# All nine depthwise taps of a convolution block on TensorE as 64x64 matmuls

## The chip, the cores and the metric

The kernel runs on one core of a Trainium2 chip. The metric is the device time of one execution in microseconds (us). A core has five engines that run side by side and meet at semaphores: TensorE (PE, matmuls and transposes, results to PSUM; PEld is its loading of weights), VectorE (DVE), ScalarE (ACT), GpSimd (POOL) and SyncE (SP), which here only issues DMA.

## The reference

The input x is 16 images of 128 channels and 28x28 pixels, all float32.

```
x = x + conv(layer_norm_over_channels(x))
   conv: h = depthwise 3x3(h) + dw_b;  h = relu(bn1(h)); a channel of an image whose max is below 4.0 becomes 0
         h = pointwise 128x128(h) + pw_b; h = relu(bn2(h)); a channel whose max is below 0.001 becomes 0
t = tokens of x: 12544 rows of 128
t = t + ffn(layer_norm_over_the_row(t))
   ffn: softmax over all tokens of t @ Wr (8 experts); each expert takes its 1024 best tokens;
        gelu(sel @ W1 + b1) @ W2 + b2, weighted with the probability, added back at the tokens' places
```

## The kernel before

There are three phases. The first, up to 213 us, takes the 16 images through norm, convolution and the routing logits; the second is a search for each expert's threshold among the tokens; the third gathers rows, runs the experts and scatters and adds. The change touches only the first.

An image lies in SBUF with channels on the 128 partitions. The first phase is a software pipeline written out by hand: `steps` calls each engine's `step(pair, u)` once for each image and some more to fill and drain, and in a step the engine works on several images, each at another stage. `image(pair, u, lag)` gives the image at a stage: lag 0 is the newest, lag 5 the oldest. Steps 6 to 13 are a hardware loop with two steps in its body, the others are written out. Semaphore counts are all that order the engines.

The stages of an image are: PE transposes it to tokens in seven tiles of 112 (L704), DVE takes statistics (L964) and small moments (L976 to L1001), ACT norms the seven tiles into `ln_tok` (L538), PE transposes them back (L769) into `psB`, ACT copies them in two parts into `x_pad`, an image with a border of zeros (L570). Then comes the depthwise convolution. A tap is one of the nine shifts of the 3x3 window. Four taps run on PE (L691): for each half of the image (14 lines, 392 pixels) four matmuls of a 128x128 diagonal matrix with the shifted view of `x_pad` add up in `psC`. Five taps run on DVE (L1009): the first per half, adding the sum in `psC` (128x392), the other four over the whole image in `conv` (128x784).

ACT then applies batch norm and relu (`act1`, L519) and sums signs to find dead channels (L509). DVE turns the sum into a flag (L1077) and masks the pointwise weights with it (`pw_masked`, L1085). PE does the pointwise product (L729), ACT norms it (`act2`, L492) and sums signs (L500), DVE adds the residual (`x1`, L1103). PE transposes `x1` to token rows in `psD` (L746) and makes the logits (L750). DVE takes statistics of the rows, ACT norms seven tiles of them (L483), and SP stores them. Matmuls of float32 appear in the trace as two records each, one after the other, and each with a weight load of its own; a transpose is one record.

On SP each step loads the input for two images later, the residual's input and a store of zeros, and stores finished rows.

## Time and profile before

| | |
|---|---|
| median of 3 runs (504.53 to 506.65) | 505.8 us |
| profiled execution, from first to last instruction | 502.9 us |
| PE, PEld busy | 361.9, 255.7 us |
| DVE, ACT, POOL busy | 327.1, 274.3, 159.3 us |
| mean granted TensorE clock | 0.857 |

The profiled execution has no timed figure of its own, only its span. What lies around the span can be taken as 2.9 us, the median less the span. A row of a group gives how often an operation ran, its busy time, the mean length of one, and the idle time in front. [...] In a timeline several instructions of one line are merged, so the time from one to the next is the length less one instruction, divided by their number less one. Matmuls are pipelined, so that a record is longer than the distance to the next.

### The profile page before, as it was taken

The numbers are of one execution on the slowest core, as the hardware profiler recorded it, in microseconds if no ns is written. First come the engines' busy times: TensorE is split into PE (matmuls) and PEld (weight loads), VectorE is DVE, ScalarE is ACT, GpSimd is POOL, SyncE is SP. The second block draws the span as 40 slices with busy tenths as digits, with TensorE's granted clock in tenths as the row PEclk, the third lists the DMA queues.
The fourth block names the chain that finished last, engine by engine and source line by source line (L and its number), as shares of the span: only waits on it lengthen the run. The fifth ranks groups of instructions, "written<-read, shape, count | busy, mean of one in ns | idle before, by whom it ended". The sixth has DMA issues, their size and how long they took to land. (4 is left out here: it accounts for less than half of the span.)

```text
span 502.9 us, 6936 instructions
## 1 busy us (share of the span) xinstructions
PE 361.9 (72%) x1947; PEld 255.7 (51%) x1947; DVE 327.1 (65%) x1004; ACT 274.3 (55%) x587; POOL 159.3 (32%) x151
## 2 busy tenths in 40 slices
PE   4989888888889985631021798999990498876575
PEld 3656555566666553520011374677560467464453
DVE  5699988888889898578879548556620025235444
ACT  3577888888888876677640528556551240510000
POOL 4000000000000000000005777787888788876000
PEclk9999999999999997655555799999997598997755
DMA  4604555555554342479101223344443267847998
GB/s 103 188 38 141 185 168 185 167 185 168 185 182 150 130 131 96 137 238 392 71 1 33 55 56 94 95 65 64 83 85 34 55 189 134 194 61 169 285 390 344
DMA packets 36396, 72.01 MB, mean 143 GB/s; under 512 B 6385, under 2 KB 16785, under 8 KB 36369
## 3 DMA queue, kind: packets, MB, share of 16 engines
q1 hardware_dynamic: 24256, 56.52, 35.0%
q0 software_dynamic: 9472, 8.66, 11.2%
q10 hardware_dynamic: 2640, 6.51, 3.3%
q8 instruction: 12, 0.20, 0.2%
q14 instruction: 16, 0.12, 0.1%
HBM read 34.96 MB, written 30.29 MB: 130 GB/s over the span
## 5 line engine op out<-in xcount | busy, mean ns | idle before, releaser
L403 POOL DMA_INDIRECT picked<-token_rows,slot_idx x32 | 31.5, 986 | 270.7 <-issue 270.4
L691 PE MATMUL psC<-x_pad,tap_diag 128*128 128x392 f32 x256 | 90.8, 498 | 6.7 <-ACT x_pad L570 5.6
L1009 DVE SCALAR_TENSOR_TENSOR conv<-x_pad,taps_w,conv 128x784 f32<-128x784 f32 x64 | 65.9, 1030 | 0.8
L691 PEld LDWEIGHTS psC<-x_pad,tap_diag 128*128 128x128 f32 x256 | 46.1, 189 | 37.0 <-DVE conv L1009 5.1
L1302 DVE TENSOR_TENSOR y_sum<-psC,b_rows 128x512 f32<-128x512 f32 x15 | 10.4, 692 | 75.2 <-PE psC L869 75.2
L869 PE MATMUL psC<-w,hid 128*128 128x128 f32 x480 | 56.6, 280 | 2.2 <-ACT hid L633 2.1
L869 PEld LDWEIGHTS psC<-w,hid 128*128 128x128 f32 x480 | 55.8, 197 | 4.6 <-issue 3.0
L613 ACT ACTIVATE picked_T<-psA 128x512 f32<-128x512 f32 x16 | 9.0, 594 | 59.9 <-PE psA L836 59.9
L426 POOL DMA_INDIRECT moe_sum_late<-y_rows,slot_idx x24 | 37.9, 1581 | 9.5 <-issue 7.0
L483 ACT ACTIVATE rows<-psD,sm 112x128 f32<-112x128 f32 x98 | 35.7, 464 | 9.3 <-DVE sm L1001 9.3
L729 PE MATMUL psB<-act,pw_masked 128*128 128x392 f32 x64 | 27.9, 563 | 17.0 <-DVE pw_masked L1085 17.0
L426 POOL DMA_INDIRECT moe_sum<-y_rows,slot_idx x24 | 37.8, 1573 | 7.3 <-issue 7.0
L633 ACT ACTIVATE hid<-psB,b_T 128x512 f32<-128x512 f32 x32 | 21.7, 685 | 31.3 <-PE psB L857 31.3
L538 ACT ACTIVATE ln_tok<-psA,sm 112x128 f32<-112x128 f32 x98 | 36.0, 501 | 0.8 <-DVE sm L1001 0.8
L857 PE MATMUL psB<-picked_T,w 128*128 128x512 f32 x64 | 32.3, 629 | 4.9 <-ACT picked_T L613 3.9
L857 PE MATMUL psC<-picked_T,w 128*128 128x512 f32 x64 | 32.2, 614 | 0.0
L964 DVE BATCH_NORM_STATS2 st<-psD 112x6 f32<-112x128 f32 x112 | 24.8, 286 | 9.5 <-PE psD L750 7.9
L633 ACT ACTIVATE hid<-psC,b_T 128x512 f32<-128x512 f32 x32 | 21.8, 687 | 15.1 <-PE psC L857 15.1
L729 PEld LDWEIGHTS psB<-act,pw_masked 128*128 128x128 f32 x64 | 12.0, 206 | 31.0 <-DVE pw_masked L1085 19.1
L797 PE MATMUL psA<-sign_sum,half_same 128*128 128x4 f16 x16 | 3.0, 188 | 34.2 <-ACT x_in L585 33.2
L964 DVE BATCH_NORM_STATS2 st<-psA 112x6 f32<-112x128 f32 x105 | 22.2, 285 | 5.6 <-PE psA L704 5.6
L1199 DVE TENSOR_SCALAR_CACHE_REDUCE conv<-dist,cand 128x784 bf16<-128x784 f32 (+1 forms) x31 | 24.6, 830 | 0.9 <-DVE cand L1217 0.5
(211 smaller groups left out, 728.8 us busy)
## 6 DMA issues: line engine op xcount, KB each, us to landing
token_rows<-rows SPq DMA_DIRECT2D x16, 416.5 KB, 3.6
x_in<-in_x_dram SPq DMA_DIRECT2D x16, 392.0 KB, 3.5
x_res<-in_x_dram SPq DMA_DIRECT2D x16, 392.0 KB, 4.3
moe_sum<-zero_rows SPq DMA_DIRECT2D x16, 392.0 KB, 4.9
x_all<-x SPq DMA_DIRECT2D x16, 392.0 KB, 2.9
moe_sum_late<-zero_rows SPq DMA_DIRECT2D x16, 392.0 KB, 7.7
out_dram<-act ACTq DMA_DIRECT2D x16, 392.0 KB, 6.2
w<-in_L_ffn_W_dram SPq DMA_DIRECT2D x16, 256.0 KB, 3.3
```

The lines of the kernel that those rows point to most:

```text
L403: nc.gpsimd.indirect_dma_start(out=picked_in[k][:, b, :], out_offset=None, in_=rows_dram, in_offset=bass.IndirectOffsetOnAxis(ap=slot_idx[ ...
L426: nc.gpsimd.indirect_dma_start(out=sums, out_offset=at, in_=y_rows[:, q, b, :], in_offset=None, compute_op=ALU.add).then_inc(s_sca[q], 16)
L483: ins = nc.scalar.activation(rows[:, q5, t * ROW:t * ROW + C], row_region(img5)[:, t, :], ACT.Identity, bias=row_sm[:, 6, t:t + 1], scale= ...
L538: ins = nc.scalar.activation(ln_tok[:, q, t * C:(t + 1) * C], ln_region(img)[:, t, :], ACT.Identity, bias=ln_sm[:, 6, t:t + 1], scale=ln_s ...
L633: nc.scalar.activation(hid[:, f, h * HS:(h + 1) * HS], hidden_bank[f], ACT.Gelu, bias=b1_T[:, ds(e * FT + f, 1)]).then_inc(s_gelu, 1)
L691: ins = nc.tensor.matmul(psC[:, h, 0:HALF].rearrange("c (h w) -> c h w", w=W), tap_diag[:, n, :], x_pad_v[:, q, y0:y0 + LINES, dx:dx + W], ...
L729: nc.tensor.matmul(psB[:, h, 0:HALF], pw_masked[:, q, :], act1[:, q, h * HALF:(h + 1) * HALF], start=True, stop=True).then_inc(s_pw, 1)
L857: nc.tensor.matmul(hidden_bank[f], w1[:, q, f * 128:(f + 1) * 128], picked_T[:, h * HS:(h + 1) * HS], start=True, stop=True).then_inc(s_l1, 1)
L869: ins = nc.tensor.matmul((psA if first else psC)[:, h, b * C:(b + 1) * C], hid[:, f, lo:lo + 128], w2[:, q, f * C:(f + 1) * C], start=(f = ...
L964: ins = nc.vector.bn_stats(st[:, lo + t, :], region[:, t, :])
L1009: return nc.vector.scalar_tensor_tensor(o, x_pad_v[:, q, y0 + dy:y0 + dy + lines, dx:dx + W], taps_w[:, PE_TAPS + n:PE_TAPS + n + 1], acc, ...
L1199: return nc.vector.tensor_scalar(junk[:, column, 0:n], dist[:, 0:n], value.bitcast(F32), -offset, ALU.is_lt, ALU.add, accum_out=cnt[:, col ...
```

## The change

The five taps on DVE and their buffers' waits go. All nine taps run on PE as 64x64 matmuls. The 128 channels are split into two halves of 64. For the upper 14 lines of the image the two halves of the channels use rows 0 to 63 of the array with columns 0 to 63, and rows 64 to 127 with columns 64 to 127. For the lower 14 lines the input lies in SBUF with the two channel halves exchanged, and the matmuls use the two other quarters of the array (rows 0 to 63 with columns 64 to 127, and the reverse), so that the result comes out at the right partitions. For each tap the four quarters follow one another: 36 matmuls per image, each over 392 pixels, where there were 8.

To have the lower half exchanged, `x_pad` becomes two parts of 17 lines. ACT copies the first 16 lines straight (L525 of the kernel after), and DVE copies the last 16 lines in two instructions, each from 64 partitions of `psB` to the other 64 of `x_turned_v`. PE transposes one tile twice for it (eight transposes in place of seven). The norm of the rows moves from ACT to DVE. `act1` now reads `psC`. At the start DVE makes 18 diagonal blocks of 128x64 in place of four of 128x128, and two more small DMAs load the exchanged taps.

The step order is new. An image's convolution is at lag 2 (it was at lag 1), the turning back and the copies are at lag 1, and its transposes to tokens at lag 0. The special regions of the first and last images are gone: norm tiles are always in `psA`, rows always in `psD`. The zeros for the stores lie in `hid`, so ACT waits for the last of these stores before the experts. SP's order is: store rows, keep x1, load the residual's input, store zeros, load the next input.

```diff
-PE_TAPS = 4
 TAPS = [(dy, dx) for dy in range(3) for dx in range(3)]
-DVE_TAPS = len(TAPS) - PE_TAPS
+HC = C // 2
+KEPT = 16
+PART = (KEPT + 1) * PW
...
-        tap_diag = sb("tap_diag", [128, PE_TAPS, 128])
+        taps_turned = sb("taps_turned", [128, 9])
+        ident_half = sb("ident_half", [128, HC])
+        tap_diag = sb("tap_diag", [128, 9, HC])
+        tap_turned = sb("tap_turned", [128, 9, HC])
...
-        x_pad = sb("x_pad", [128, 2, (H + 2) * PW])
+        x_pad = sb("x_pad", [128, 2, 2 * PART])
...
+        zero_rows = hid[0:P, 0, 0:TPI * C]
...
-        x_pad_v = x_pad[:, :, :].rearrange("c q (h w) -> c q h w", w=PW)
+        x_pad_v = x_pad[:, :, 0:PART].rearrange("c q (h w) -> c q h w", w=PW)
+        x_turned_v = x_pad[:, :, PART:2 * PART].rearrange("c q (h w) -> c q h w", w=PW)
...
-                def norm_rows():
-                    act.wait_ge(s_sc, img5 + 6)
-                    if since(img5, 2):
-                        act.wait_ge(s_rows[q5], use5 * 16)
-                    for t in range(TPI):
-                        ins = nc.scalar.activation(rows[:, q5, t * ROW:t * ROW + C], row_region(img5)[:, t, :], ACT.Identity,
-                                                   bias=row_sm[:, 6, t:t + 1], scale=row_sm[:, 5, t:t + 1])
-                    ins.then_inc(s_n3, 1)
...
+                    act.wait_ge(s_conv, img2 + 1)
+                    if since(img2, 2):
+                        act.wait_ge(s_pw, img2 * 2 - 2)
+                    nc.scalar.activation(act1[:, q2, :].rearrange("c (h n) -> c h n", n=HALF), psC[:, :, 0:HALF], ACT.Relu,
+                                         bias=fold[:, 8:9], scale=fold[:, 4:5]).then_inc(s_h1, 1)
...
+                    act.wait_ge(s_t2, img1 * 2 + 1)
+                    nc.scalar.activation(x_pad_v[:, q1, 1:1 + KEPT, 1:1 + W],
+                                         psB[:, 0, 0:KEPT * W].rearrange("c (h w) -> c h w", w=W), ACT.Copy).then_inc(s_pad, 1)
...
+            def conv_taps(img, q):
+                pe.wait_ge(s_pad, img + 1)
+                pe.wait_ge(s_turn, img + 1)
+                if isinstance(img, int) and img == 0:
+                    pe.wait_ge(s_setup, 1)
                 if since(img, 1):
-                    pe.wait_ge(s_taken, img * 2 + h - 1)
-                for n in range(PE_TAPS):
+                    pe.wait_ge(s_h1, img)
+                pe.sem_inc(s_pe, 1)
+                for n in range(9):
                     dy, dx = TAPS[n]
-                    y0 = h * LINES + dy
-                    ins = nc.tensor.matmul(psC[:, h, 0:HALF].rearrange("c (h w) -> c h w", w=W), tap_diag[:, n, :],
-                                           x_pad_v[:, q, y0:y0 + LINES, dx:dx + W],
-                                           start=(n == 0), stop=(n == PE_TAPS - 1))
+                    for half, weights, lines in ((0, tap_diag, x_pad_v), (1, tap_turned, x_turned_v)):
+                        for row in range(2):
+                            of = slice(row * HC, row * HC + HC)
+                            col = row if half == 0 else 1 - row
+                            y0 = dy + half
+                            ins = nc.tensor.matmul(psC[col * HC:col * HC + HC, half, 0:HALF].rearrange("c (h w) -> c h w", w=W),
+                                                   weights[of, n, :], lines[of, q, y0:y0 + LINES, dx:dx + W],
+                                                   start=(n == 0), stop=(n == 8))
                 ins.then_inc(s_conv, 1)
...
+                    for a, tiles in enumerate((range(4), range(3, TPI))):
+                        pe.wait_ge(s_n1, img * 2 + a + 1)
+                        for n, t in enumerate(tiles):
+                            ins = nc.tensor.transpose(psB[:, a, n * P:(n + 1) * P],
+                                                      ln_tok[:, q, t * C:(t + 1) * C], ident[0:P, 0:P])
+                        ins.then_inc(s_t2, 1)
...
-            def tap(q, n, h, first):
-                dy, dx = TAPS[PE_TAPS + n]
-                y0, lines = (h * LINES, LINES) if first else (0, H)
-                o = conv[:, q, y0 * W:(y0 + lines) * W].rearrange("c (h w) -> c h w", w=W)
-                acc = psC[:, h, 0:HALF].rearrange("c (h w) -> c h w", w=W) if first else o
-                return nc.vector.scalar_tensor_tensor(o, x_pad_v[:, q, y0 + dy:y0 + dy + lines, dx:dx + W],
-                                                      taps_w[:, PE_TAPS + n:PE_TAPS + n + 1], acc, ALU.mult, ALU.add)
...
+                for n in range(9):
+                    nc.vector.tensor_scalar(tap_diag[:, n, :], ident_half[:, :], taps_w[:, n:n + 1], None, ALU.mult)
+                    nc.vector.tensor_scalar(tap_turned[:, n, :], ident_half[:, :], taps_turned[:, n:n + 1], None, ALU.mult)
...
+                    dve.wait_ge(s_sc, k)
+                    for t in range(TPI):
+                        ins = nc.vector.tensor_scalar(rows[:, q5, t * ROW:t * ROW + C], row_tiles[:, t, :],
+                                                      row_sm[:, 5, t:t + 1], row_sm[:, 6, t:t + 1], ALU.mult, ALU.add)
+                    ins.then_inc(s_n3, 1)
...
+                if on0:
+                    stats(ln_tiles, 0, s_m1, img0, s_t1)
+                if on1:
+                    dve.wait_ge(s_t2, img1 * 2 + 2)
+                    if since(img1, 2):
+                        dve.wait_ge(s_conv, img1 - 1)
+                    for to, of in ((0, HC), (HC, 0)):
+                        ins = nc.vector.tensor_copy(x_turned_v[to:to + HC, q1, 0:KEPT, 1:1 + W],
+                                                    psB[of:of + HC, 1, 0:KEPT * W].rearrange("c (h w) -> c h w", w=W))
+                    ins.then_inc(s_turn, 1)
```

PE over one step before. L691 is one half's taps, L729 the pointwise product, L746 and L750 rows and logits, L704 the transposes to tokens, L769 the turning back.

```order
L691 MATMUL psC<-x_pad,tap_diag 128x392 x4
L729 MATMUL psB<-act,pw_masked 128x392 x2
L746 MATMUL psD<-ident,x 112x128 x7
L750 MATMUL psD<-wr_c,x 112x8 x7
L704 MATMUL psA<-ident,x_in 112x128 x7
L691 MATMUL psC<-x_pad,tap_diag 128x392 x4
L769 MATMUL psB<-ident,ln_tok 128x112 x7
```

PE after, over the end of one step and the start of the next. L653 is the convolution, L681, L695, L707, L711 and L669 are the lines that were L704, L769, L746, L750 and L729.

```order
L653 MATMUL psC<-x_pad,tap_turned 64x392 x2
L681 MATMUL psA<-ident,x_in 112x128 x7
L695 MATMUL psB<-ident,ln_tok 128x112 x8
L707 MATMUL psD<-ident,x 112x128 x7
L711 MATMUL psD<-wr_c,x 112x8 x7
L669 MATMUL psB<-act,pw_masked 128x392 x2
L653 MATMUL psC<-x_pad,tap_diag 64x392 x2
L653 MATMUL psC<-x_pad,tap_turned 64x392 x2
```

What moved: the convolution is one block behind the pointwise product, where it was in two halves with the rows, logits and transposes between them. Nine pairs of the L653 rows stand in each step.

DVE over one step before. L1009 are the taps, L1077 and L1085 the flag and the masked weights, L964 the statistics of rows (`psD`) and of tokens (`psA`).

```order
L996 RECIPROCAL sm<-sm 112x14
L1118 TENSOR_TENSOR logits<-psD,sm 112x7x8
L1121 TENSOR_TENSOR rows<-psD,sm 112x7x8
L1001 SCALAR_TENSOR_TENSOR sm<-sm 112x14
L1009 SCALAR_TENSOR_TENSOR conv<-x_pad,taps_w,conv 128x784
L1077 TENSOR_SCALAR keep<-keep 128x1
L1085 TENSOR_SCALAR pw_masked<-pw_T,keep 128x128
L1009 SCALAR_TENSOR_TENSOR conv<-x_pad,taps_w,conv 128x784 x2
L964 BN_STATS st<-psD 112x6 x7
L1009 SCALAR_TENSOR_TENSOR conv<-x_pad,taps_w,conv 128x784
L964 BN_STATS st<-psA 112x6 x7
```

DVE after, over one step. L1015 norms the rows, L1037 are the copies of the lower half, L1043 and L1049 the flag and the masked weights.

```order
L938 RECIPROCAL sm<-sm 112x14
L943 SCALAR_TENSOR_TENSOR sm<-sm 112x14
L1008 TENSOR_TENSOR logits<-psD,sm 112x7x8
L1011 TENSOR_TENSOR rows<-psD,sm 112x7x8
L1015 TENSOR_SCALAR rows<-psD,sm 112x128 x7
L1021 TENSOR_SCALAR keep<-keep 128x1
L1027 SCALAR_TENSOR_TENSOR x<-act,keep,x_res 128x784
L906 BN_STATS st<-psA 112x6 x7
L1037 COPY x_pad<-psB 64x16x28 x2
L1043 TENSOR_SCALAR keep<-keep 128x1
L1049 TENSOR_SCALAR pw_masked<-pw_T,keep 128x128
L906 BN_STATS st<-psD 112x6 x7
```

What moved: the masked weights, which the pointwise product waits for, stood early in a step among the taps and now stand late, behind the token statistics and the copies.

## Rows read from the trace of the kernel before

**Rows 1.** The page, part 2: busy tenths in 40 slices of 12.57 us.
```profile
PE   4989888888889985631021798999990498876575
DVE  5699988888889898578879548556620025235444
...
PEclk9999999999999997655555799999997598997755
```

**Rows 2.** Stretches, us: length, busy (instructions) PE, PEld, DVE, ACT, POOL; clock, DMA.
```profile
96.00:108.00 12.00, 10.73 (x57) 7.27 (x56) 10.70 (x34) 10.38 (x27) 0.00 (x0) 1.00 0.52 169
...
240.00:503.00 263.00, 178.27 (x1030) 130.25 (x1030) 128.36 (x346) 89.41 (x144) 154.19 (x128) 0.80 0.49 121
```

**Rows 3.** Timeline of PE over one step: start us, length us, what.
```profile
95.50 2.90 PE L691 MATMUL psC<-x_pad,tap_diag 128*128 128x392 f32 x8 [0.42 <-ACT x_pad L570]
99.24 1.58 PE L729 MATMUL psB<-act,pw_masked 128*128 128x392 f32 x4 [0.84 <-DVE pw_masked L1085]
100.66 0.93 PE L746 MATMUL psD<-ident,x 128*112 128x128 f32 x7
101.43 1.45 PE L750 MATMUL psD<-wr_c,x 128*112 128x8 f32 x14
102.73 0.95 PE L704 MATMUL psA<-ident,x_in 128*112 128x128 f32 x7
103.52 2.80 PE L691 MATMUL psC<-x_pad,tap_diag 128*128 128x392 f32 x8
106.16 0.84 PE L769 MATMUL psB<-ident,ln_tok 112*128 112x112 f32 x7
107.42 2.90 PE L691 MATMUL psC<-x_pad,tap_diag 128*128 128x392 f32 x8 [0.43 <-ACT x_pad L570]
```

**Rows 4.** Groups by shape, 60 to 180 us: busy us, mean ns, idle before.
```profile
L691 PE MATMUL psC<-x_pad,tap_diag 128*128 128x392 f32 x166 | 59.3, 499 | 4.7 <-ACT x_pad L570 4.7
L1009 DVE SCALAR_TENSOR_TENSOR conv<-x_pad,taps_w,conv 128x784 f32<-128x784 f32 x40 | 41.2, 1029 | 0.4
...
L1009 DVE SCALAR_TENSOR_TENSOR conv<-x_pad,taps_w,psC 128x392 f32<-128x392 f32 x21 | 13.0, 617 | 0.0
...
L483 ACT ACTIVATE rows<-psD,sm 112x128 f32<-112x128 f32 x70 | 25.5, 465 | 8.1 <-DVE sm L1001 8.1
...
L492 ACT ACTIVATE act<-psB,fold 128x392 f32<-128x392 f32 x20 | 13.3, 760 | 0.0
L519 ACT ACTIVATE act<-conv,fold 128x784 f32<-128x784 f32 x10 | 10.3, 1026 | 0.0
...
L509 ACT ACTIVATE signs<-act,limits 128x784 bf16<-128x784 f32 x10 | 9.4, 942 | 0.0
...
L1085 DVE TENSOR_SCALAR pw_masked<-pw_T,keep 128x128 f32<-128x128 f32 x10 | 2.9, 286 | 1.2
...
L1077 DVE TENSOR_SCALAR keep<-keep 128x1 f32<-128x1 f32 x10 | 1.5, 147 | 0.0
```

**Rows 5.** Timeline of the start: first norm, setup, turning and convolution.
```profile
8.65 2.55 ACT L538 ACTIVATE ln_tok<-psA,sm 112x128 f32<-112x128 f32 x7 [0.38 <-DVE sm L1001]
9.19 0.87 DVE L1046 TENSOR_SCALAR tap_diag<-ident,taps_w 128x128 f32<-128x128 f32 x4
...
11.77 1.57 PE L769 MATMUL psB<-ident,ln_tok 112*128 112x112 f32 x7
...
14.54 5.43 PE L691 MATMUL psC<-x_pad,tap_diag 128*128 128x392 f32 x16
```

**Rows 6.** Timeline from the last pointwise product into the search.
```profile
200.73 2.98 PE L729 MATMUL psB<-act,pw_masked 128*128 128x392 f32 x4 [3.45 <-DVE pw_masked L1085]
...
213.60 1.54 PE L781 MATMUL psA<-ident,logits 112*128 112x112 f32 x7 [4.34 <-ACT rows L483]
...
217.95 0.69 DVE L1190 TENSOR_SCALAR dist<-psA,mcol 128x448 f32<-128x448 f32 x1
...
218.56 0.56 DVE L1191 TENSOR_SCALAR dist<-psA,mcol 128x336 f32<-128x336 f32 x1
```

More of the change, by code:

```diff
@@ L730, in step @@
                                          start=True, stop=True).then_inc(s_pw, 1)
[L731 removed]
+                on, img, q, _ = image(pair, u, 2)
                 if on:
[L733 to L743 removed]
+                    conv_taps(img, q)
@@ new lines, in step @@
+                on, img, q, use = image(pair, u, 0)
+                if on:
+                    pe.wait_ge(s_xin[q], use * 16 + 16)
+                    for a, tiles in enumerate(BANK_TILES):
+                        if since(img, 1):
+                            pe.wait_ge(s_n1, img * 2 + a - 1)
+                        for t in tiles:
+                            ins = nc.tensor.transpose(ln_tiles[:, t, :], x_in[:, q, t * P:(t + 1) * P], ident[:, :])
+                        ins.then_inc(s_t1, 1)
@@ L1087, in step @@
[L1087 to L1093 removed]
+                if on1 or on5:
+                    now = columns(on1, on5)
+                    inverse(img1 if on1 else None, img5 if on5 else None, now)
+                    shift(k - 1, now)
@@ L1171, in _ @@
+                if on4:
+                    stats(row_tiles, TPI, s_m3, img4, s_t3)
+                if on0 or on4:
+                    new = columns(on0, on4)
+                    moments_a(img0 if on0 else None, img4 if on4 else None, new)
+                    moments_b(k, new)
+                    moments_c(k, new)
+                if isinstance(img0, int) and img0 == 0:
+                    setup_first()
             steps(dve, step)
```

391 lines of the change are left out of this document (122 added, 269 removed).

## The prediction

> **What bounds the kernel now.** I read the page's slices first. For the first 14 of 40 slices PE and DVE both stand at 8 or 9 tenths at full clock [rows 1]: the first phase is bound by two engines that are nearly equally full. The table of stretches says the same in numbers: of 12.00 us in the middle, PE is busy 10.73, DVE 10.70 and ACT 10.38 [rows 2]. The 263 us behind 240 belong to the search's end and the experts [rows 2], which the change leaves alone.
>
> Then comes one step in the timeline of PE. The same L691 block starts at 95.50 and at 107.42, so a step takes 11.92 us [rows 3]. Of these PE waits 0.84 for the masked weights and 0.43 for the padded image [rows 3]; the rest, 10.65, is work. The step is therefore a sum on PE with small waits. From one start to the next the other blocks take: pointwise product 1.42 (99.24 to 100.66), row transposes 0.77, logits 1.30, transposes to tokens 0.79 [rows 3]. Turning back is seven tiles in 0.84 [rows 3], 0.12 each with the tail. The convolution is two halves of 2.64 (103.52 to 106.16) [rows 3], 5.3 us in all.
>
> **The price of a record.** A float32 matmul of 392 columns is two records. Eight records run from 103.52 to the next block at 106.16, so the distance is 0.330 us; the eight of 95.50 last 2.90, which less one record of 0.492 and over seven is 0.344 [rows 3, 4]. [...] I take 0.337, their mean.
>
> The change makes 36 matmuls or 72 records per image. Everything hangs on how many run beside one another, which no row of this trace shows, since every L691 record here fills the array. The ends are these. One after another: 72 x 0.337 = 24.3 us per image. Four at a time: 18 x 0.337 = 6.1 us. Between them lies a case that comes from how a matmul is split. Its two records use the same quarter of the array, so the second can't begin before the first is through. If the engine starts records strictly in program order, the next matmul's first record can only start with the second record of this one. Two records then overlap at any time: 36 x 0.337 = 12.1 us.
>
> The rows show that records go in order, with the second of a matmul one distance behind the first [rows 3, 4], and show no start out of order. That is why I take 12.1, the middle value, and keep 6.1 and 24.3 as ends.
>
> [...]
>
> **What else changes on PE.** Turning back has eight tiles, 0.96 us. So a step is 1.42 + 0.79 + 0.96 + 0.77 + 1.30 = 5.24 us beside the convolution.
>
> **DVE.** It loses four taps of 1.03 and two of 0.62, 5.4 us per step [rows 4]. It gains two copies of 64x448 from PSUM and seven norms of 128 columns. The nearest row to a copy is the 128x448 operation from PSUM, 0.69, with the next one 0.61 behind it [rows 6]: 1.2 to 1.4 for both. A norm lies between the 0.20 distance of the four 128x128 operations [rows 5] and 0.31, which the line through 448 at 0.69 and 336 at 0.56 [rows 6] gives for 128 columns: 1.4 to 2.2 for seven, I take 1.8. DVE ends near 10.7 - 5.4 + 1.3 + 1.8 = 8.4 us. ACT loses the 25.5 us over 10 steps of row norms, 2.55 per step [rows 4], and one of two copies. Neither is a bound any more.
>
> **The new wait.** The pointwise product waits for the masked weights, which are now late. After the convolution's end PE does 0.79 + 0.96 = 1.75 us of transposes, then DVE makes two copies, 1.3, then the flag and the mask, 0.15 + 0.29 [rows 4], with about 0.2 of handoffs: 3.7 us. In the same time PE does the rows and logits too, 3.82 us. ACT's side, `act1` 1.03 and signs 0.94 [rows 4] and the reading of their sum, about as long as the flag, is ready by 2.3. The wait is covered by the rows and logits, with 0.1 to spare; I count 0.25 for it and for the handoffs per step. Queued behind the waiting product on PE is the whole next convolution, so if the copies take 1.4 and handoffs more, it costs 0.3 per step. A step is 5.5 us plus the convolution.
>
> **Start.** The first convolution starts at 14.54 [rows 5]. The transposes of image 1 now use `psA` and so wait for the norm of image 0, which ends at 11.2 (8.65 + 2.55); with 1.57 for turning back [rows 5] and as much for them it is 14.3. DVE makes 18 blocks at up to 0.20 in place of four in 0.87 [rows 5], which puts its statistics and copies to 16.8. I take 17.0, against 14.54.
>
> **End.** After the last convolution `act1`, signs, flag and mask take 2.9 us. From the last pointwise product to the search's first transposes it was 213.60 - 200.73 = 12.9 us [rows 6]. Now rows have one PSUM region, and their norm stands on DVE in front of the last statistics: 1.8 and 0.8 of handoffs more, 15.5. Together 18.4.
>
> **Sum.** With X for the convolution of an image: start 17.0; 16 X; after the first one 5.3 (there are no rows yet); 14 steps of 5.5, 77.0; less 0.8 for the step without new tokens; end 18.4. The search then begins at 116.9 + 16 X instead of 213.6. Behind it nothing changes: ACT's wait for the stores of zeros is over long before the experts. The span becomes 502.9 - 213.6 + 116.9 + 16 X = 406.2 + 16 X. With X = 12.1 that is 599.8, and with the 2.9 us between span and median 602.7. Rounded, **603 us**. At the two distances, 0.330 and 0.344, X is 11.9 and 12.4, and the time 599 to 608.
>
> **The rivals.**
>
> *Four at a time, 508 us.* If the engine holds a matmul's second record back at its quarter and goes on to the next quarter, X = 6.1 to 6.2 and the time is 409.1 + 16 x 6.2 = 508. For it: the four quarters are all different within a tap. Against it: records in order, as above. Its lower bound is X = 5.9, 504; its upper bound comes from how fast records can be issued. L750 has 14 tiny records, each with its load, in 1.30 us [rows 3], 0.093 each; 72 of them are 6.7 us, 516.
>
> *Four at a time, and PE never waits, 496 us.* This is the faster side. A step becomes 5.24 + 5.9, 11.15 us instead of 11.92. That needs the mask to be ready before PE ends the logits: 3.82 us behind the convolution. From 3.6 us down it holds. It saves 0.25 x 14 = 3.5 against the last rival; with X at 5.9 another 5, and with norms on DVE at 1.4 and a start at 15, 3 more: 508 - 12 = 496. For it: the 1.27 us of waits of now are waits on DVE and ACT [rows 3], and both get lighter. Against it: the mask comes late by the new order.
>
> *One after another, 798 us.* The change then doesn't do what it says: the 64x64 matmuls don't overlap at all. 409.1 + 16 x 24.3 = 798. For it: no row shows an overlap of two matmuls beyond the tail of a record. Against it: nothing in the trace ties two different quarters together, only order. A convolution in pairs at the lower of the two clocks, if the chip granted less to a half-used array, would look the same in time. The cold product of four records takes 2.98 against 1.58 [rows 3, 6], a factor of nearly two.
>
> *Pairs with more around them, up to 640.* Each of the 36 matmuls changes the quarter; 0.06 us for each would be 35 us.
>
> **How the numbers follow.** Pairs 0.50, four with waits 0.22, four without waits 0.10, one after another 0.12, pairs with more 0.06. The time is the likeliest case's, 603, whose own range is 597 to 612. The range for 8 in 10 has to take in both four-at-a-time cases: 496 to 620. It leaves out one after another and half of the last case, 0.15. No change is within 0.5% of 505.8, 503.3 to 508.3, which is about what a measurement of this kernel can tell. Faster: the third case and almost nothing of the second, 0.10. Same: somewhat under half of the second, 0.10. Slower: 0.80.
>
> **What would show it.** In the profile after, the distance between starts of two L653 records: 0.17 us is pairs, 0.085 four at a time, 0.34 one after another. The convolution block per step lasts 12, 6 or 24 us. PE stands at 9 tenths through the first phase at full clock, DVE at 5 (at 7 if four at a time). The search's first transposes start near 311 (216 with four). The wait of the pointwise product for the mask should be under 0.4 per step. The mean record of L653 would stay near 0.5. The prediction is wrong if the granted clock falls below 1.0 in the convolution, if the distance is 0.085, or if a step outside the convolution is not near 5.5.

## The result, and the profile after

The changed kernel takes 520.7 us (median of 4 runs, 518.2 to 522.4) against 506.2 for the kernel before on the same chip (4 runs, 504.5 to 507.4): a ratio of 1.0295, 95% interval 1.0247 to 1.0343. Three executions were slower than the rest of their kernel, two of them at a lower granted clock (0.549 and 0.816, where the others beside them had 0.837 to 0.859), and the medians and ratios here leave them out. The change makes the kernel slower, as forecast, but by 15 us and not by 97 (603 less 505.8). The profiled execution has a span of 520.6 us, 17.7 more than before.

The convolution itself came out at the fastest end of its bounds. Here is PE's timeline of one step, with start and length in us; the lines left out repeat the pattern.

```profile
102.55 1.58 PE L669 MATMUL psB<-act,pw_masked 128*128 128x392 f32 x4 [0.41 <-DVE pw_masked L1049]
104.06 0.55 PE L653 MATMUL psC<-x_pad,tap_diag 64*64 64x392 f32 x2
104.07 0.55 PE L653 MATMUL psC<-x_pad,tap_turned 64*64 64x392 f32 x2
104.44 0.49 PE L653 MATMUL psC<-x_pad,tap_diag 64*64 64x392 f32 x2
...
110.14 0.98 PE L681 MATMUL psA<-ident,x_in 128*112 128x128 f32 x7
110.96 0.93 PE L695 MATMUL psB<-ident,ln_tok 112*128 112x112 f32 x8
111.72 0.93 PE L707 MATMUL psD<-ident,x 128*112 128x128 f32 x7
112.49 1.45 PE L711 MATMUL psD<-wr_c,x 128*112 128x8 f32 x14
114.53 0.92 PE L669 MATMUL psB<-act,pw_masked 128*128 128x392 f32 x2 [0.59 <-DVE pw_masked L1049]
```

Four records, one in each quarter, start within 0.02 us. The next four start 0.38 later, then the distance is 0.33, and 0.44 from the last four to the transposes. So 72 records take 18 distances: 104.06 to 110.14 is 6.08 us. A step is 11.98 (from the product at 102.55 to that at 114.53), where it was 11.92 [rows 3]. All that DVE gave up bought nothing, because PE works longer than before: 11.4 us of a step (11.98 less 0.59) where it was 10.65. The shorter waits, 0.41 to 0.59 for the mask in place of 1.27 in all [rows 3], give back only as much as the longer work takes.

The groups by shape between 60 and 180 us (busy us, mean ns | idle before) show what PE waits for. L653 also has a second group of 362 for `tap_turned`, with the same times:

```profile
L653 PE MATMUL psC<-x_pad,tap_diag 64*64 64x392 f32 x362 | 62.3, 493 | 0.0
L1015 DVE TENSOR_SCALAR rows<-psD,sm 112x128 f32<-112x128 f32 x71 | 23.6, 402 | 0.2 <-issue 0.2
L669 PE MATMUL psB<-act,pw_masked 128*128 128x392 f32 x40 | 17.1, 553 | 4.6 <-DVE pw_masked L1049 4.6
L1037 DVE COPY x_pad<-psB 64x448 f32<-64x448 f32 x20 | 12.5, 624 | 0.5
```

A record of 64x64 is about as long (493 ns) as one of 128x128 was (499, [rows 4]). The mask costs 4.6 us in ten steps. The row norms on DVE take 2.3 us a step.

The stretches give length, busy time (instructions) of PE, PEld, DVE, ACT, POOL, then the granted clock, the DMA share and GB/s:

```profile
42.00:44.00 2.00, 2.00 (x8) 0.73 (x11) 0.30 (x2) 1.04 (x2) 0.00 (x0) 0.73 0.04 8
44.00:50.00 6.00, 6.00 (x64) 2.48 (x60) 1.56 (x4) 3.90 (x11) 0.00 (x0) 0.80 0.36 102
96.00:108.00 12.00, 11.59 (x120) 7.11 (x116) 9.50 (x38) 7.75 (x19) 0.00 (x0) 1.00 0.52 169
138.00:144.00 6.00, 5.62 (x36) 2.36 (x40) 3.69 (x20) 3.38 (x9) 0.00 (x0) 0.72 0.27 105
```

Against [rows 2], PE rose from 10.73 to 11.59 of 12 us, DVE fell only from 10.70 to 9.50, ACT from 10.38 to 7.75. Twice, around 44 and around 140 us, the granted clock falls from the 1.00 of the stretch at 96, to a mean of 0.72 to 0.80 over these stretches; inside them it is 0.50 from 43.5 to 46.2 and 0.52 from 138.4 to 141.2. The steps there last 13.27 and 13.45 us, not the 11.6 to 12.0 of the steps around them.

The end, where it was 12.9 us from the last pointwise product to the search [rows 6], is 20.9:

```profile
207.74 1.58 PE L669 MATMUL psB<-act,pw_masked 128*128 128x392 f32 x4 [0.60 <-DVE pw_masked L1049]
213.19 1.39 PE L707 MATMUL psD<-ident,x 128*112 128x128 f32 x7 [3.87 <-DVE rows L1015]
214.38 2.64 PE L711 MATMUL psD<-wr_c,x 128*112 128x8 f32 x14
221.83 1.74 PE L707 MATMUL psD<-ident,x 128*112 128x128 f32 x7 [4.81 <-DVE rows L1015]
223.36 2.65 PE L711 MATMUL psD<-wr_c,x 128*112 128x8 f32 x14
228.63 1.54 PE L723 MATMUL psA<-ident,logits 112*128 112x112 f32 x7 [2.62 <-issue]
```

The last two images share the one region `psD`. Each must wait until DVE has normed the rows of the image before, and behind such a wait PE's matmuls run at about half speed (2.64 for what takes 1.45 in a step; the granted clock is 0.55 from 213.2 to 217.0 and 0.50 from 221.8 to 226.0).

So the 17.7 us of span are: 15.0 at the start of the search (228.63 against 213.60) and 2.7 behind it. Of the 15.0, 8.0 stand in the end, 3.3 in the 13 steps from the pointwise product of image 2 to that of image 15 (152.7 against 149.4 us), 4.8 between the products of images 0 and 2 (24.9 against 20.1), and -1.1 in the start. Of the 2.7, 0.45 lie at the transpose of `bmax` behind the search's first transposes. The rest arises behind the last gather; I did not follow it.

### The profile page after: what moved, and what is told of

It reads as the page before. It is cut to its first block and busy times, and to the rows that moved or that the text cites. A ratio compares the mean times of both kernels' runs of the same rounds, so it can differ in the third digit from the quotient of the medians.

```text
span 520.6 us, 8608 instructions
## 1 busy us (share of the span) xinstructions
PE 381.8 (73%) x2859; PEld 255.6 (49%) x2859; DVE 306.8 (59%) x1060; ACT 229.9 (44%) x459; POOL 159.3 (31%) x151
## 3 DMA queue, kind: packets, MB, share of 16 engines
q0 software_dynamic: 9472, 8.66, 11.1%
## 5 line engine op out<-in xcount | busy, mean ns | idle before, releaser
L653 PE MATMUL psC<-x_pad,tap_diag 64*64 64x392 f32 x576 | 102.4, 507 | 3.1 <-DVE x_pad L1037 3.1
L653 PE MATMUL psC<-x_pad,tap_turned 64*64 64x392 f32 x576 | 102.4, 507 | 0.0
L653 PEld LDWEIGHTS psC<-x_pad,tap_diag 64*64 64x64 f32 x576 | 40.3, 137 | 60.6 <-issue 60.6
L906 DVE BATCH_NORM_STATS2 st<-psA 112x6 f32<-112x128 f32 x112 | 23.8, 284 | 35.6 <-PE psA L681 35.6
L496 ACT ACTIVATE ln_tok<-psA,sm 112x128 f32<-112x128 f32 x112 | 40.5, 456 | 0.6 <-DVE sm L943 0.6
L653 PEld LDWEIGHTS psC<-x_pad,tap_turned 64*64 64x64 f32 x576 | 40.0, 137 | 0.0
L799 PE MATMUL psB<-picked_T,w 128*128 128x512 f32 x64 | 34.1, 660 | 5.3 <-ACT picked_T L564 4.3
L469 ACT ACTIVATE act<-psB,fold 128x392 f32<-128x392 f32 x32 | 21.1, 677 | 38.1 <-PE psB L669 38.1
L1015 DVE TENSOR_SCALAR rows<-psD,sm 112x128 f32<-112x128 f32 x112 | 37.0, 402 | 0.2 <-issue 0.2
L669 PE MATMUL psB<-act,pw_masked 128*128 128x392 f32 x64 | 26.9, 544 | 10.2 <-DVE pw_masked L1049 10.2
L510 ACT ACTIVATE act<-psC,fold 128x784 f32<-128x784 f32 x16 | 16.1, 1005 | 34.8 <-PE psC L653 34.8
```

Source lines behind the costliest of these rows:

```text
L469: nc.scalar.activation(act2[:, q3, h * HALF:(h + 1) * HALF], psB[:, h, 0:HALF], ACT.Relu, bias=fold[:, 9:10], scale=fold[:, 5:6]).then_inc ...
L496: ins = nc.scalar.activation(ln_tok[:, q1, t * C:(t + 1) * C], ln_tiles[:, t, :], ACT.Identity, bias=ln_sm[:, 6, t:t + 1], scale=ln_sm[:, ...
L510: nc.scalar.activation(act1[:, q2, :].rearrange("c (h n) -> c h n", n=HALF), psC[:, :, 0:HALF], ACT.Relu, bias=fold[:, 8:9], scale=fold[:, ...
L653: ins = nc.tensor.matmul(psC[col * HC:col * HC + HC, half, 0:HALF].rearrange("c (h w) -> c h w", w=W), weights[of, n, :], lines[of, q, y0: ...
L669: nc.tensor.matmul(psB[:, h, 0:HALF], pw_masked[:, q, :], act1[:, q, h * HALF:(h + 1) * HALF], start=True, stop=True).then_inc(s_pw, 1)
L799: nc.tensor.matmul(hidden_bank[f], w1[:, q, f * 128:(f + 1) * 128], picked_T[:, h * HS:(h + 1) * HS], start=True, stop=True).then_inc(s_l1, 1)
```

## The experiments

Each kernel is the changed one with the edit shown. The edits are shortened: `(...)` and `[...]` stand for what is left out, and so do comments in place of code. Ratios are against the kernel before, run on the same chip in turns.

### 1. The order in which quarters get their records

**Nine taps of one quarter before the next.**

```diff
-for n in range(9):
-    for half, weights, lines in (...):
-        for row in range(2):
+for half, weights, lines in (...):
+    for row in range(2):
+        for n in range(9):
```

> The kernel after, with the same 36 matmuls per image in another order: all nine taps of one quarter of the array, then the next quarter. Theory A (records are started in program order, or nearly so, and four run together only because neighbouring matmuls use four different quarters): with 18 records of one quarter in front of the next quarter's, the convolution takes up to 72 x 0.33 = 24 us per image and the kernel some 800 us. Theory B (each quarter has its own queue, as deep as these 18 records and their loads): four run together still, about 520 us. Anything between tells how deep the engine looks: with a few matmuls of look-ahead the blocks overlap only at their edges, 700 to 800 us.

Measured: 753.3 us (2 runs), ratio 1.492 (1.484 to 1.499). PE's timeline of one convolution:

```profile
133.84 9.81 PE L653 MATMUL psC<-x_pad,tap_diag 64*64 64x392 f32 x33
143.17 0.54 PE L653 MATMUL psC<-x_pad,tap_turned 64*64 64x392 f32 x1
143.50 0.49 PE L653 MATMUL psC<-x_pad,tap_diag 64*64 64x392 f32 x1
...
143.83 0.49 PE L653 MATMUL psC<-x_pad,tap_diag 64*64 64x392 f32 x1
...
144.16 0.49 PE L653 MATMUL psC<-x_pad,tap_diag 64*64 64x392 f32 x1
144.21 9.76 PE L653 MATMUL psC<-x_pad,tap_turned 64*64 64x392 f32 x33
153.91 0.97 PE L681 MATMUL psA<-ident,x_in 128*112 128x128 f32 x7
```

The four quarters do not run together in this order: the block is 20.07 us, 61 distances of 0.33. But look at 143.17. The first record of the third quarter (`tap_turned`) starts, and three `tap_diag` records that stand ahead of it in the program start after it. So records are not started in the program's order. I read it so that a quarter that is busy holds some of its own, and the engine goes on past them. Strict order would give 69 distances (17 per quarter and one at the end), 22.7 us. A queue of four per quarter, the running record included, gives 60; that is a model of mine, worked out from the program's order, and not something that the trace shows directly.

**Three taps, and two taps, per quarter at a time.**

```diff
-for n in range(9):
-    for half, weights, lines in (...):
-        for row in range(2):
+for n0 in range(0, 9, 3):            # in the second kernel: range(0, 9, 2)
+    for half, weights, lines in (...):
+        for row in range(2):
+            for n in range(n0, n0 + 3):   # min(9, n0 + 2)
```

> The changed kernel with its 36 matmuls in blocks of three taps: quarter 1 takes taps 0 to 2, then quarter 2, 3 and 4 theirs, then taps 3 to 5, and so on. Same matmuls, other order. With 0.33 us a record: Theory A (a quarter holds about 4 records of its own, running one included, and the engine goes on past it until the next record for a full quarter): 28 record times in a row, a block of 9.2 us, a step 3.3 us longer, a time near 573. Theory B (about 4 waiting records for all quarters together): 33 record times, 10.9 us, a time near 600. Theory C, that of the prediction (no record may begin before the one ahead of it in the program): 61 record times, 20.1 us, a time near 750.

> The changed kernel with its conv in blocks of two taps per quarter, so four records of a quarter stand one behind the other before the next quarter's. The blocks of three left open whether the records that wait are counted per quarter (28 record times expected) or over all (33): it took 29.8. Theory A (about four per quarter, the running one included): 18 record times as in the changed kernel, the block stays near 6.0 us, the time 519 to 523. Theory B (about four over all quarters): 21 record times, the step 1.0 us longer, near 537. Theory C (a window of four to six records of the program's order that may be under way): 28 to 36 record times, over 560.

Measured: three taps 583.5 us (2 runs), ratio 1.155 (1.149 to 1.160). Two taps 523.0 us (4 runs), ratio 1.033 (1.027 to 1.039). The time of three taps lies between theory A's 573 and theory B's 600, nearer to A. Here are start and end of a block of each, three taps first:

```profile
210.25 1.91 PE L654 MATMUL psC<-x_pad,tap_diag 64*64 64x392 f32 x8
211.68 0.54 PE L654 MATMUL psC<-x_pad,tap_turned 64*64 64x392 f32 x1
211.95 0.55 PE L654 MATMUL psC<-x_pad,tap_diag 64*64 64x392 f32 x2
...
220.24 0.98 PE L682 MATMUL psA<-ident,x_in 128*112 128x128 f32 x7
```

```profile
105.30 0.55 PE L654 MATMUL psC<-x_pad,tap_diag 64*64 64x392 f32 x2
105.32 0.55 PE L654 MATMUL psC<-x_pad,tap_turned 64*64 64x392 f32 x2
...
111.54 0.98 PE L682 MATMUL psA<-ident,x_in 128*112 128x128 f32 x7
```

With two taps (four records of a quarter in a row) the block is 6.24 us against 6.08, and all four quarters start at once: close to theory A's 18 distances, and far from the 53 of strict order, worked out like the others. With three taps (six in a row) it is 9.99 us; less the 0.14 that the block of the changed kernel has over 18 distances, that is 29.8 distances, where per-quarter queues of four give 28, one common queue of four 33, and strict order 61. Strict order is refuted by all three kernels. Among models of this kind, a queue of four per quarter fits best: three per quarter would give 63, 39 and 21 distances for nine, three and two taps, five per quarter 57, 21 and 18, four per quarter 60, 28 and 18, and measured are 60.4, 29.8 and 18.5. It is 1.8 short in one of them, so what the engine really does stays open.

**Does a quarter cost anything while others run?** The lower half computes one tap of nine here, so 20 matmuls instead of 36.

```diff
         for half, weights, lines in (...):
+            if half and n:
+                continue
```

> The kernel after, with eight of the nine taps of the lower half left out, so that the convolution has 20 matmuls per image in place of 36, in two quarters of the array for eight of nine taps. Theory A (a quarter streams its own records, 0.33 us each, whatever the others do): the block still takes 18 x 0.33 = 5.9 us and the time stays at 518 to 521. Rival (the four share one stream of 0.083 us per record, or the issue of records is the limit): the block takes 40 x 0.083 = 3.3 us, and the time is about 16 x 2.6 = 42 us less, 478, or 490 if the wait for the masked weights takes a part of it.

Measured: 520.0 us (2 runs), ratio 1.030 (1.024 to 1.036). The block stays 6.08 us long (102.90 to 108.98) with two records every 0.33. Taking 16 matmuls away saves nothing: the two quarters of the upper half still have 18 records each, and these follow one another at the same 0.33.

**36 matmuls of 64x64 as 18 of 128x128.**

```diff
+for half, lines in ((0, x_pad_v), (1, x_turned_v)):
+    for n in range(9):
+        nc.tensor.matmul(psC[:, half, ...], tap_full[:, n, :], lines[...], ...)
```

> The changed kernel, but with 18 matmuls of 128x128 per image in place of 36 of 64x64 (both channel halves in one, the lower half copied without exchange); so 36 records where four quarters had 18 beside each other. Theory A (what bounds the conv is the number of records that follow each other on one part of the array, 0.33 us each): a block of 36 x 0.33 = 11.9 us, steps near 17.5 us, and with 16 images a time of 605 to 620. Rival B (the block is bound by what feeds the array, four times as many columns read in the changed kernel as here): the block is 6 to 9 us and the time under 570.

Measured: 608.8 us (2 runs), ratio 1.205 (1.199 to 1.210). PE's timeline of one block:

```profile
210.69 1.58 PE L665 MATMUL psB<-act,pw_masked 128*128 128x392 f32 x4 [0.28 <-DVE pw_masked L1045]
212.11 12.02 PE L649 MATMUL psC<-x_pad,tap_full 128*128 128x392 f32 x36
223.96 0.93 PE L677 MATMUL psA<-ident,x_in 128*112 128x128 f32 x7
```

36 records one after another are 11.85 us (212.11 to 223.96), 0.33 each. The block is as theory A has it, and so is the time. Cutting into quarters is worth half of the convolution. The 608.8 is also very nearly the 603 that I had forecast, since pairs of records on quarters would have had the same 36 distances.

### 2. What the step lost beside the convolution

**Row norms back on ACT.**

```diff
+            # ACT, behind the norm of the tokens
+            act.wait_ge(s_rl, img5 + 1)
+            for t in range(TPI):
+                ins = nc.scalar.activation(rows[...], row_tiles[:, t, :], ...)
-            # the seven tensor_scalar of DVE (L1015)
```

> The kernel after, with the norm of the rows back on ACT, behind its norm of the tokens. Theory A (most of the loss is at the end of the first phase, where rows of images 14 and 15 share one PSUM region, so that statistics, moments, inverse and norm of one stand in front of the transposes of the next, on whichever engine they run): the norm on ACT takes about 2.55 us where DVE took 2.31 in the same chain, so the time stays within 519 to 522 us, and the search's first transposes stay near 228.6. Theory B (the norms cost because DVE runs them in its own queue in front of the residual sum): the end gets 2 x 2.3 us shorter and each step's residual comes earlier, 514 to 516 us.

Measured: 521.0 us (4 runs), ratio 1.030 (1.023 to 1.037); steps of 11.99 and 11.81 us as in the changed kernel. The time is as theory A has it. In the steps the largest new item on DVE costs nothing: DVE reaches it behind the mask, and afterwards waits for PE's next transposes to tokens in any case, 1.1 to 1.2 us with the norms and 3.1 to 3.2 without them. In the end it does not get shorter either, but 1.2 us longer (product at 208.40, search at 230.52, not near 228.6), with the norms on ACT in the same chain.

**One of the two copies of the lower half on ACT.**

```diff
+            # ACT, behind its own copy
+            nc.scalar.activation(x_turned_v[HC:C, ...], psB[0:HC, 1, ...], ACT.Copy)
-            for to, of in ((0, HC), (HC, 0)):     # DVE
+            for to, of in ((0, HC),):
```

> The kernel after, with one of the two copies of the lower half moved from DVE to ACT, where it stands behind the copy of the upper half. Theory A (the product waits for the masked weights because DVE makes them behind both copies; 0.4 to 0.6 us per step in the loop, 0.23 outside, 2.28 in the two steps of the filling): the masked weights come 0.63 us earlier. That saves 8 x 0.5 + 4 x 0.23 + 3 x 0.63, about 6.5 us: 513 to 515 us, and a step of the loop falls from 11.98 to about 11.45. Rival (ACT's queue, now longer by 0.55 us, or the register instructions of DVE's loop are what ends last): 519 to 521 us.

Measured: 510.5 us (10 runs), ratio 1.0087 (1.0053 to 1.0121), a gain of 10 us, more than theory A's 6.5. PE's timeline, then two stretches of the same kernel:

```profile
106.47 1.56 PE L672 MATMUL psB<-act,pw_masked 128*128 128x392 f32 x4
114.06 0.98 PE L684 MATMUL psA<-ident,x_in 128*112 128x128 f32 x7
...
117.71 1.56 PE L672 MATMUL psB<-act,pw_masked 128*128 128x392 f32 x4
```

```profile
36.00:50.00 14.00, 12.37 (x125) 7.91 (x122) 7.17 (x30) 10.79 (x22) 0.00 (x0) 1.00 0.58 186
138.00:156.00 18.00, 18.00 (x180) 11.30 (x182) 14.34 (x62) 13.56 (x32) 0.00 (x0) 1.00 0.58 190
```

In the steps no wait is left: from 138 to 156 us PE is busy without a gap, and a step is 11.24 us. The two steps of the filling still wait 1.60 and 1.63, now for ACT's copies, and the last product 0.60. The clock stays at 1.0 in both stretches where it had fallen. In the two profiled executions the search starts 10.8 us earlier (217.87 against 228.63), and 3.3 of these are the two steps at half clock, which theory A had not counted; whether they went because of the copy is not shown (see *What the half clock comes from*).

### 3. The end, and all together

**Regions of their own for the last rows.**

```diff
+last_tiles = psC[0:P, :, :].rearrange("p a (t c) -> p (a t) c", c=C)
+def row_region(img):      # rows of 14 in psA, of 15 in psC, else psD
+    return {B - 2: ln_tiles, B - 1: last_tiles}.get(img, row_tiles) if isinstance(img, int) else row_tiles
```

> The changed kernel, with the transposes of the last rows in regions of their own again: image 14 in psA, image 15 in psC. Theory A (the longer end is the wait for the one region psD: transposes of rows(14) stand 3.87 us and those of rows(15) 4.81 us behind the norms of the image before): both waits go, from the pw-product of image 15 to the search 20.9 us become 13 to 15, and the time is 513 to 515. Rival B (the end is one chain on VectorE, whose instructions would stand behind each other in any region): the waits turn into waits for the statistics, the stretch stays above 18.5 us, and the time is 518 to 521.

Measured: 516.2 us (4 runs), ratio 1.021 (1.016 to 1.026). PE's timeline of the end:

```profile
207.81 1.58 PE L675 MATMUL psB<-act,pw_masked 128*128 128x392 f32 x4 [0.60 <-DVE pw_masked L1059]
...
214.48 1.71 PE L717 MATMUL psC<-ident,x 128*112 128x128 f32 x7 [3.04 <-DVE x L1037]
...
223.02 1.54 PE L733 MATMUL psA<-ident,logits 112*128 112x112 f32 x7 [4.39 <-issue]
```

Both waits for the row norms are gone and the end is 15.2 us, not 20.9. The stretch is near theory A, the time between the two: it fell by 4.5 us. The end is still 2.3 us longer than in the kernel before. I read that as DVE's chain, in which the row norms of images 13 and 14 stand with 2.3 us each (those of image 15 run beside the search); the next kernel takes them off.

**Together**: one copy on ACT, last rows apart, row norms of images 13 to 15 on ACT, and a changed start. There the exchanged taps are loaded behind the input of image 1, so DVE begins on the other parameters without them, and the search's constants are made behind the first copy of the lower half. The matrices of the exchanged taps are still built in front of that copy (11.31 to 12.86 us, the copy at 14.29), other than the expectation below says.

```diff
-dve.wait_ge(s_prm, 16 * 13)
+dve.wait_ge(s_prm, 16 * 11)
+                dve.wait_ge(s_prm2, 32)     # between the nine tap_diag and the nine tap_turned
+                # behind the first copy: setup_late(), the constants of the search
+            # norms of the rows of images 13 to 15 on ACT, from row_region(img5)
+            if on5 and isinstance(img5, int) and img5 >= B - 3:
```

> Together: the second copy of the lower half on ScalarE, the last rows in regions of their own (image 14 in psA, 15 in psC), the norms of the rows of images 13 to 15 on ScalarE, and a start in which the exchanged taps are loaded behind the input of image 1 and their matrices built behind the first copy. From the 509.7 us span with the copy on ScalarE: the end shorter by 6 to 8 us, the start by 1 to 1.5. Theory A (start, mask wait and end add up, each on the chain): 500 to 503 us, so faster than the kernel before by about 1%. Rival B (the end is bound by VectorE's chain whatever the region): 507 to 509, no faster than before.

Measured: 497.8 us (6 runs, 496.6 to 498.9), ratio 0.9851 (0.9823 to 0.9879). It beats the kernel before by 1.5%, with an interval wholly below 1, and the changed kernel by 23 us. It is also below theory A's 500 to 503. Against the kernel with the copy moved, the first product comes 3.7 us earlier (24.45, it was 28.11), where I had counted 1 to 1.5, and the end is 11.1 us shorter (11.5, it was 22.6), where I had counted 6 to 8. PE's timeline:

```profile
15.02 0.55 PE L671 MATMUL psC<-x_pad,tap_diag 64*64 64x392 f32 x2 [1.42 <-DVE x_pad L1065]
...
24.45 1.55 PE L687 MATMUL psB<-act,pw_masked 128*128 128x392 f32 x4 [1.60 <-ACT x_pad L543]
...
191.63 1.58 PE L687 MATMUL psB<-act,pw_masked 128*128 128x392 f32 x4 [0.60 <-DVE pw_masked L1079]
...
203.13 1.54 PE L745 MATMUL psA<-ident,logits 112*128 112x112 f32 x7 [3.60 <-ACT rows L515]
```

The first convolution starts at 15.02 (17.65 in the changed kernel) and runs at full speed (6.09 us to the next block, where it was 8.44), the end is 11.5 us, and the search starts 10.5 us before that of the kernel before (213.60, [rows 6]). Two more kernels take one part back each.

```diff
 # e9: together, but with the start of the changed kernel
-dve.wait_ge(s_prm, 16 * 11)
+dve.wait_ge(s_prm, 16 * 13)
 # e10: together, but with both copies on DVE
-for to, of in ((0, HC),):
+for to, of in ((0, HC), (HC, 0)):
```

> The combined version without its changed start (parameters, exchanged taps and their matrices as in the changed kernel). In the combined version the first pw-product begins at 24.45 us, in the one with only the copy moved at 28.11. Theory A (the start stands on the chain and adds up with the rest): the search begins 3.7 us later than 203.1, the time is 501 to 502.5. Rival B (the later steps take back what the start loses, as one engine always has slack there): the search within 1 us of 203.1, the time 497 to 499.

> The combined version with both copies of the lower half on VectorE again. Theory A (the mask's products stand behind the copies on VectorE: 0.41 to 0.59 us of waiting per step in the loop and 0.7 us more in each filling step): steps of 11.8 and 12.0 us instead of 11.24, 13 of them, so 8 to 10 us more, and with two steps at half clock, as the changed kernel has them, 11 to 13 more: 506 to 511 us, no faster than the kernel before. Rival B (the copies cost only while norms of rows and copies meet on VectorE): under 501 us. If the two steps at half clock come from the 2.28 us waits of the filling steps, they come here too; if from what the start does, they are gone.

Measured: without the start 499.3 us (3 runs, 497.6 to 502.3), ratio 0.985 (0.978 to 0.992). In its profiled execution the search starts 5.9 us later (209.04) than in the combined version: 2.0 from a later first convolution (17.04), 2.8 because that convolution runs its first groups at half speed, and 1.1 in the end. That speaks for theory A, but the ratios of the two kernels do not differ, so whether the start saves time overall stays open. With two copies on DVE 508.1 us (9 runs, 503.6 to 510.3), ratio 1.0044 (1.0007 to 1.0081), within theory A: steps of 11.8 and 12.0 again, and the end still short (12.66). So the copy is worth about 10 us in the combined version (1.0044 less 0.9851, of 506). Of the two slow steps the first came back, behind the same two waits of 2.28 us, and the second did not:

```profile
36.00:50.00 14.00, 11.72 (x101) 5.91 (x100) 6.04 (x25) 8.04 (x18) 0.00 (x0) 0.88 0.48 153
130.00:156.00 26.00, 24.99 (x252) 15.32 (x245) 19.67 (x74) 15.79 (x35) 0.00 (x0) 1.00 0.54 173
```

## Why the prediction was right in direction and wrong in size

**The step that failed** is the one that set X, the convolution per image: "If the engine starts records strictly in program order, the next matmul's first record can only start with the second record of this one." From that came X = 12.1 where 5.94 was measured, and 16 times the 6.2 too much is 99 us. That is more than the whole error: the span was to be 599.8 and is 520.6. The other terms took 19 back. That a record on 64 rows and columns is no closer to the next than one of 128x128 was my assumption, without a row. The runs show it: 6.08 us is 18 distances of 0.33 on quarters, 11.85 is 36 of 0.33 with 128x128, and a record takes 493 ns against 499 [rows 4]. The rest of the reasoning on X held too: each quarter needs 18 distances, as it would if the second record of a matmul waits for the first, and taking 16 of the 36 matmuls away leaves the block at 6.08. What was wrong is that nothing behind a waiting record could start. I had no row on that point and chose the middle of the bounds (6.1 to 24.3); the nearest rows show records in order on the full array (128x128, [rows 3]) and none on quarters, so they could not bear on it.

**Around the block.** The product before the block has 1.51 us to the next start where it was 1.42 [rows 3], and the block has 6.08 for 18 x 0.33 = 5.94. Together 0.23 us per step, 3.7 over 16 images, which had no place in my sum. The kernel with 128x128 matmuls in the convolution has neither: 1.42 from product to block (210.69 to 212.11), and 11.85 for 36 distances of 0.33. What the 0.23 comes from no run shows.

**The terms beside X.** With the measured X = 5.94 my sum is a span of 406.2 + 95.0 = 501.2; measured 520.6, so 19.4 us were missing. With the 2.9 between span and median my sum would have said 504, no slower than before. That the kernel came out slower at all is due to the terms below, which I had too small, so the direction was in part luck.

| term | predicted | measured | off |
|---|---|---|---|
| first convolution starts | 17.0 | 17.65 | +0.65 |
| first to second convolution (X + 5.3) | 11.2 | 14.0 | +2.7, of it 2.4 at half speed |
| 14 steps to the convolution of image 15 | 159.4 | 167.2 | +7.8 |
| that convolution to the last product (X + 2.9) | 8.8 | 8.9 | +0.1 |
| last product to search | 15.5 | 20.9 | +5.4 |
| behind the search | 289.3 | 292.0 | +2.7 |

*Start*: right to 0.65. DVE's 18 blocks came 0.16 apart, below my 0.20. The first seven groups of the convolution run at half speed:

```profile
17.65 0.92 PE L653 MATMUL psC<-x_pad,tap_diag 64*64 64x392 f32 x2 [3.06 <-DVE x_pad L1037]
...
18.33 0.89 PE L653 MATMUL psC<-x_pad,tap_diag 64*64 64x392 f32 x2
```

They are 0.65 apart in place of 0.33, behind a wait of 3.06. The profile's clock reads 1.00 here, so that it is the clock is not shown in this run; in the kernel with one copy moved, groups of the first convolution that are 0.65 apart have a granted clock of 0.50 (18.0 to 21.3 us). I saw such a slow product in [rows 6] (in the profile before the granted clock is 0.50 from 200.7 to 203.7) and left it out of the start.

*Steps*: the mask's wait is 0.41 and 0.59, where I had 0.25. I had a chain of 3.7 against 3.8 of cover and said that 0.3 more would show. The chain is 4.39: 110.14, where the convolution ends, to the product at 114.53. DVE's timeline has it:

```profile
110.83 1.48 DVE L906 BATCH_NORM_STATS2 st<-psA 112x6 f32<-112x128 f32 x7 [1.18 <-PE psA L681]
112.34 1.26 DVE L1037 COPY x_pad<-psB 64x448 f32<-64x448 f32 x2
113.63 0.15 DVE L1043 TENSOR_SCALAR keep<-keep 128x1 f32<-128x1 f32 x1
113.91 0.29 DVE L1049 TENSOR_SCALAR pw_masked<-pw_T,keep 128x128 f32<-128x128 f32 x1
```

I let the copies start when PE had turned the image back, 1.75 us behind the convolution. But on DVE they stand behind the statistics of the tokens, 1.5 us, which can't begin before PE's transposes to tokens; so they start 2.20 behind it. That is 0.45 of the 0.7, a term that my chain left out. The one step of the last images without new tokens bears it out: no statistics stand there, and its product (197.29) waits for nothing. The copies took 1.26 for two, within my 1.2 to 1.4; the rest, 0.26, is in flag, mask and handoffs (0.90 from 113.63 to 114.53, where I had 0.64). Moving one copy gave the 0.25 and more back, and 11.24 is within 0.1 of the 11.15 that I gave for steps without waits. The two steps at half clock, 1.6 each, had no place in the sum; they are 3.3 of the 7.8, and the 0.23 around each block another 3.2; the rest is the mask's waits and small terms.

*End*: the mechanism was right (one region, norms on DVE), its size was not. I charged one norm; there were two waits in a row, 3.87 and 4.81, and matmuls at half clock behind them, 1.2 each.

**The rivals.** *Four at a time, 508* had the right mechanism and a chance of 0.22; it missed by 12.7 us for the terms above. *No waits, 496* is about what the combined version reached, 497.8, but only with all four of its edits. *One after another, 798* is nearly the fate of the same 36 matmuls in another order: 753. DVE was to go to 8.4; it is 9.5, and norms at 2.3 a step against my 1.8 are 0.5 of that, the rest I did not follow. Of the signs that I had named for a wrong prediction, all three came: 72 records in 6.08 us are 0.084 each, the granted clock is 0.50 in the convolution at 43.5 us, and a step has 5.9 us beside its convolution (11.98 less 6.08) where I had 5.5. The search's first transposes start at 228.6, where I had 311, and 216 for four at a time. The range, 496 to 620, held the time; it had been drawn so wide because it had to take in both mechanisms. The 0.06 us for each change of quarter, in *pairs with more around them*, was a guess without a row; measured is 0.23 us around a whole block of 36 matmuls.

**What the half clock comes from** is open. Behind the two waits of 2.28 in the filling the next step is slow in the changed kernel and in those with the norms on ACT, the last rows apart and two taps (granted clock 0.50 from 44 to 46 us), three taps (0.50 from 50 to 53) and two copies (0.50 from 40 to 43). The kernels with 1.60 and 1.63 there have no slow step (1.00 from 30 to 55). But the kernel with 20 matmuls waits the same 2.28 twice and has none (11.62 us, granted clock 1.00 from 42 to 54), so these waits alone don't decide it. The second slow step moves: it begins at 138.38 in the changed kernel, at 114.64 with the last rows apart, and is absent with two taps and with two copies, though all four have the same waits of 0.4 to 0.6 in their steps. Each profile is one execution, and no run singles the cause out.

## What to carry to other kernels

Small matmuls can run beside each other on the quarters of the array, but the order in which the program issues them decides it: the block of 36 took 6.08 us with one matmul per quarter in turn, 6.24 with two, 9.99 with three and 20.07 with nine. So for matmuls as here, go round the quarters with at most two each (four records of float32). Time that one engine gives up is no gain until the engine that was nearly as full gives up some too (DVE fell from 10.70 to 9.50 us of 12, and the step stayed at 11.98 where it was 11.92); here all that shortened the changed kernel were the mask's chain, the first images and the last. Where two bounds lie a factor of four apart and no row is near, the middle is not safer than the ends, and it hides that the answer was one of two mechanisms.

## What the runs showed that I had not expected

A quarter that is busy does not stop the others: in one order the first record of the third quarter started at 143.17 and three that stand ahead of it at 143.50 to 144.16, and a model that holds up to four at each quarter fits three orders best (60, 28 and 18 distances, measured 60.4, 29.8 and 18.5). Cutting 128x128 matmuls with diagonal weights into four sets of 64x64 halves the convolution (11.85 to 6.08 us), though it doubles the matmuls. The block of 64x64 matmuls has a price around it that shows only beside the kernel with 128x128: 0.23 us per block. And single steps ran in part at half clock (granted 0.50, 13.27 us against 11.6 to 12.0), in some kernels and not in another with the same waits.
